# Block 0's tile masks packed four groups to a word, score masks moved between scores, and the last normalisation finished on ScalarE

## The reference

```python
# block 0
qkv = (layer_norm(x, ln1_g, ln1_b) @ Wqkv + bqkv).reshape(N, 3, H, DH)       # N = 625, H = 8, DH = 64
a = einsum('ehd,ehd->eh', q[src] * D ** -0.5, k[dst]) + dist_attn + path_attn
e = exp(a - segment_max(a, dst)[dst]); sa = e / segment_sum(e, dst)[dst]
agg = segment_sum(v[src] * sa[:, :, None], dst)
h1 = x + agg @ Wo + bo; block0 = h1 + gelu(layer_norm(h1) @ W1 + b1) @ W2 + b2
# block 1: 4 layers of sparse attention + MLP; block 2: hidden MLP and a sum over edges
# block 3: 8 attention heads over the edges, and then
x = (x + block3 - mean) / sqrt(var + 1e-5)                                     # the output, 625 x 512
```

## Time and profile before

| what | us |
|---|---|
| median of 3 runs | 1360.0 (1359.12 to 1360.21) |
| the profiled execution | 1355.65 |
| its span | 1353.7 |
| PE busy | 1161.8 (86% of the span) |
| DVE busy | 871.6 (64%) |
| POOL busy | 268.5 (20%) |
| ACT busy | 456.7 (34%) |

### The profile page before, as it was taken

How to read it: one execution, slowest core, us unless ns; L and a number is a source line. 1 busy time by engine, 2 the same in 40 slices (tenths; PEclk the granted TensorE clock), 3 DMA queues, 4 the chain that set the end, 5 groups by cost and what they waited for, 6 DMA issues and landing times.

```text
span 1353.7 us, 15095 instructions
## 1 busy us (share of the span) xinstructions
PE 1161.8 (86%) x5730; PEld 884.6 (65%) x5730; DVE 871.6 (64%) x1536; ACT 456.7 (34%) x673; POOL 268.5 (20%) x313
## 2 busy tenths in 40 slices
PE   5987845667889997899999999999999999879983
PEld 2654523334458975897779877898779877646552
DVE  6686745545644258566776667667766568937885
ACT  1010640000014432435325343336235342216780
POOL 1266338888600001000110000000110001110001
PEclk9988877788889998899999999999999999778897
DMA  6255883222151143020010201121010321000001
GB/s 181 61 150 152 278 258 81 46 52 67 18 163 56 33 130 105 4 101 25 32 62 4 101 23 63 32 65 61 31 60 3 101 62 54 16 0 1 0 1 38
DMA packets 47903, 93.95 MB, mean 69 GB/s; under 512 B 17200, under 2 KB 17600, under 8 KB 46418
## 3 DMA queue, kind: packets, MB, share of 16 engines
q1 hardware_dynamic: 27338, 71.77, 16.8%
q0 software_dynamic: 20480, 20.99, 6.5%
HBM read 74.65 MB, written 17.91 MB: 68 GB/s over the span
## 4 chain that ended last, share of the span: by engine, by line
PE 63%; DVE 14%; POOL 10%; ACT 5%; issue 4%; DMA 3%; SPq 0%; POOLq 0%; DVEq 0%; ACTq 0%
PE ps L1481 16%; PE ps L1534 15%; PE ps L1509 10%; POOL logit_ring L601 6%; PE ps L1514 5%; PE ps L1568 4%; POOL arena L595 3%; PE ps L1639 2%; PE ps L1668 2%; DMA logits_scratch<-arena 2%; PE ps L1497 2%; DVE weight_low L1171 1%; PE ps L1614 1%; DVE arena L933 1%; ACT arena L794 1%
## 5 line engine op out<-in xcount | busy, mean ns | idle before, releaser
L1481 PE MATMUL ps<-arena 125*128 125x314 f32 (+5 forms) x820 | 228.4, 459 | 11.1 <-DVE neg_max L1040 7.1
L1481 PEld LDWEIGHTS ps<-arena 125*128 125x128 f32 (+5 forms) x820 | 143.1, 188 | 85.9 <-DVE neg_max L1040 13.5
L579 POOL TENSOR_TENSOR var_eps<-mean_var,ln_consts 125x1 f32<-125x1 f32 x70 | 15.6, 222 | 919.1 <-DVE mean_var L1187 564.9
L1639 PE MATMUL ps<-arena 125*125 125x512 f32 x192 | 120.6, 722 | 68.0 <-DVE arena L1069 62.0
L595 POOL DMA_INDIRECT arena<-value_scratch,src_idx x80 | 101.6, 1270 | 72.9 <-DMA logits_scratch<-arena 32.7
L601 POOL DMA_INDIRECT logit_ring<-logits_scratch,pair_idx x80 | 107.4, 1343 | 24.4 <-issue 24.1
L1568 PE MATMUL ps<-ident,arena 125*125 125x125 f32 x625 | 81.0, 284 | 15.6 <-ACT arena L870 7.7
L1568 PEld LDWEIGHTS ps<-ident,arena 125*125 125x125 f32 x625 | 75.9, 195 | 25.0 <-ACT arena L870 8.9
L1639 PEld LDWEIGHTS ps<-arena 125*125 125x125 f32 x192 | 32.9, 215 | 70.2 <-issue 69.8
L1640 PEld LDWEIGHTS ps<-arena 125*125 125x125 f32 x192 | 40.3, 210 | 55.6 <-issue 55.6
L1509 PE MATMUL ps<-input_high,weight_high 128*128 128x314 f32 x320 | 73.0, 309 | 2.7 <-DVE weight_low L1171 2.7
(11 more groups left out here) (267 smaller groups left out, 2655.9 us busy)
## 6 DMA issues: line engine op xcount, KB each, us to landing
logits_scratch<-arena SPq DMA_DIRECT2D x5, 2187.5 KB
arena<-in_m_w SPq DMA_DIRECT2D x8, 1024.0 KB, 6.5
arena<-in_w_up SPq DMA_DIRECT2D x4, 1024.0 KB, 8.3
arena<-in_w_down SPq DMA_DIRECT2D x4, 1024.0 KB, 10.1
arena<-in_wq SPq DMA_DIRECT2D x4, 1024.0 KB, 5.2
arena<-in_wk SPq DMA_DIRECT2D x4, 1024.0 KB, 5.1
arena<-in_wv SPq DMA_DIRECT2D x4, 1024.0 KB, 5.4
arena<-in_wo SPq DMA_DIRECT2D x4, 1024.0 KB, 5.3
```

Of the source, the lines that this page charges most:

```text
L1481: last = mm(out_view[:, place:place + HALF_W], w, r[:, lo:lo + HALF_W], start=n == 0, stop=n == len(pairs) - 1 and not open_end)
L1639: mm(ps[0:TILE, 512 * j:512 * j + 512], onehot, VG[slot][:, u, :], start=False, stop=True, skip_group_check=True)
```

## The change

1. The 5-bit words of four neighbouring groups are put into one word of 20 bits (`mask_word`, four more small Vector instructions), and TensorE's stream loads a word once in four groups, in the count loop and in the message loop. The branches stay; they test another bit.
2. Of the five score masks only the first is made before the scores. Masks 1 to 4 are made on the Vector engine between the first four heads' scores and that of head 4, in tile 0.
3. In the last normalisation GpSimd makes mean times rstd after the two power instructions, ScalarE negates it and applies scale and shift to the tile, and the Vector engine's pass over the tile goes. The output is stored for tiles 0 and 1, 2 and 3, and 4 as each is ready.

```diff
@@ sync
-            sp.wait_ge(sig("out_ready"), NT)
-            node_transfer(rows_view(out), X, "out_stored")
-            sp.wait_ge(sig("out_stored"), 32)
+            for pair in PAIRS:
+                sp.wait_ge(sig("out_ready"), pair[-1] + 1)
+                tiles = slice(pair[0], pair[-1] + 1)
+                node_transfer(rows_view(out)[:, tiles, :], X[:, tiles, :], "out_stored")
+            sp.wait_ge(sig("out_stored"), 32 * len(PAIRS))
@@ gpsimd
-            for n in range(3):
+            for n in range(2):
                 powers((sig("var_ready3"), sig("rstd_ready3")), pool_chain, n * NT)
+            for t in range(NT):
+                pool.wait_ge(sig("var_ready3"), 2 * NT + t + 1)
+                pool_chain(pool, g.tensor_tensor(vare[:, t:t + 1], mv[:, t, 1:2], lnc[:, 0:1], ALU.add))
+                pool_chain(pool, g.tensor_tensor(rstd[:, t:t + 1], vare[:, t:t + 1], lnc[:, 1:2], ALU.pow))
+                g.tensor_tensor(centre[:, t:t + 1], mv[:, t, 0:1], rstd[:, t:t + 1], ALU.mult).then_inc(sig("centre_ready"), 1)
@@ scalar
+            for t in range(NT):
+                act.wait_ge(sig("centre_ready"), t + 1)
+                a.activation(shift[:, t:t + 1], centre[:, t:t + 1], ACT.Copy, scale=-1.0).then_inc(sig("shift_ready"), 1)
+                act.wait_ge(sig("shift_ready"), t + 1)
+                a.activation(X[:, t, :], X[:, t, :], ACT.Identity, bias=shift[:, t:t + 1], scale=rstd[:, t:t + 1]).then_inc(sig("out_ready"), 1)
@@ vector
-            v.tensor_copy(mask_i[:, :], mask_f[:, :]).then_inc(sig("mask_ready"), 1)
+            of_four = mask_f[:, :].rearrange("p (w k) -> p w k", k=4)
+            dve_chain(dve, v.tensor_copy(mask_word[:, :], of_four[:, :, 3]))
+            for k in (2, 1, 0):
+                dve_chain(dve, v.scalar_tensor_tensor(mask_word[:, :], mask_word[:, :], float(1 << NT), of_four[:, :, k], ALU.mult, ALU.add))
+            v.tensor_copy(mask_i[:, :], mask_word[:, :]).then_inc(sig("mask_ready"), 1)
...
-            for j in range(NT):
+            def score_mask(j):
                 dve.wait_ge(sig("counts_ready"), j + 1)
                 dve_chain(dve, v.tensor_scalar(MASK[:, j, :], C2[:, j, :], 0.5, -BIG, ALU.is_lt, ALU.mult))
-            dve.sem_inc(sig("masks_ready"), 1)
-
+
+            score_mask(0)
             for n in range(NT * H0):
                 j, h = divmod(n, H0)
+                if j == 0 and 1 <= h < NT:
+                    score_mask(h)
+                    if h == NT - 1:
+                        dve.sem_inc(sig("masks_ready"), 1)
                 A.wait_filled(dve, ("s", j, h))
...
-            norm(back, 2 * NT, X, block3_end, done=sig("out_ready"))
+            for t in range(NT):
+                block3_end(t)
+                dve_chain(dve, v.bn_stats(stats[:, t, :], X[:, t, :]))
+                v.bn_aggr(mv[:, t, :], stats[:, t, :]).then_inc(sig("var_ready3"), 1)
@@ tensor
+            def mask_of_four(group):
+                return pe.value_load(mask_i[0:1, group // 4:group // 4 + 1], min_val=0, max_val=(1 << 4 * NT) - 1)
+
+            def reached(word, group, j):
+                return (word & (1 << (NT * (group % 4) + j))) > 0
...
             for group in range(GROUPS):
-                reached = pe.value_load(mask_i[0:1, group:group + 1], min_val=0, max_val=(1 << NT) - 1)
+                if group % 4 == 0:
+                    word = mask_of_four(group)
                 pe.wait_ge(sig("onehot_ready"), group + 1)
                 for j in range(NT):
-                    with pe.If((reached & (1 << j)) > 0):
+                    with pe.If(reached(word, group, j)):
...
```

More of the change, by code:

```diff
@@ L290, in build @@
         vare = sbuf("var_eps", [TILE, NT])
+        centre = sbuf("mean_rstd", [TILE, NT])
         lnc = sbuf("ln_consts", [TILE, 2])
+        shift = sbuf("minus_mean_rstd", [TILE, NT])
         negm = sbuf("neg_max", [TILE, 2, NT])
@@ L305, in build @@
         mask_f = sbuf("group_mask_f", [1, GROUPS])
-        mask_i = sbuf("group_mask", [1, GROUPS], i32)
+        mask_word = sbuf("mask_word_f", [1, GROUPS // 4])
+        mask_i = sbuf("mask_words", [1, GROUPS // 4], i32)
         fw1 = sbuf("f_w1", [2 * NFREQ, COND])
```

## The result

| | before | after |
|---|---|---|
| timed runs, median of 3 | 1360.0 us (1359.12 to 1360.21) | 1346.05 us (1345.98 to 1346.53) |
| the profiled execution | 1355.65 | 1346.53 |
| its span | 1353.7 | 1344.7 |
| PE, DVE, ACT, POOL busy | 1161.8, 871.6, 456.7, 268.5 | 1161.8, 869.9, 462.3, 266.3 |

The changed kernel is faster: the ratio of the times on record is 0.9915, 95% interval [0.9886, 0.9944]. This ratio is an estimate of its own and not the quotient of the two medians, which is 1346.05 / 1360.0 = 0.9897.

The account below looks back on a forecast made before the run. The prediction took TensorE's instruction stream to pace the count loop, feeding block 0's chain of stores and gathers, then TensorE's own work. Terms −4.8 + 1.7 − 4.5 = −7.6 took 1360.0 to 1352.4 us, range 1349.2 to 1357.3.

Parts of the forecast that it names:

- What bounds the kernel: Block 0: TensorE's instruction stream paces the count loop; time won or lost between counts and first store reaches the gathers.
- The mask words: Count loop: fifteen fewer loads at 0.63 us, until the last one-hots limit it; −4.8 us, nothing from the message loop.
- The score masks: First scores: masks 1 to 4, now between scores, delay the first store of logits by 1.7 us net.
- The rival that the stores hide it: First stores of logits: stores, not scores, set the pace, so the masks cost nothing; 1350.7 us, chance 0.14.
- The end, flight: Last output store: 250 KB in place of 1250 KB takes 2.5 us after issue, not 5.95; −3.45 us.
- The rival of a last store that keeps its length: End of kernel: the small last store takes as long as before, the end gives only −1.5; 1355.4 us, chance 0.09.
- The end, Vector engine and ScalarE: Last normalisation: three L915 fewer save 1.65 us, the path through ScalarE adds 0.6; last store issued 1.05 us earlier.
- The rival on gathers that stretch: GpSimd's 80 logit gathers slow beside Vector work, from mean 1.343 us; at 1.50 the time is 1365.0 us; chance 0.04.
- The base, and the width of the range: Whole kernel: timed median stays 4.35 us above the profiled execution; 8-in-10 range 1349.2 to 1357.3, with 0.8 for run spread.

Follow-up runs that it names:

- the later sets: The changed kernel measured twice more without edit, beside the kernel before: 1349.67 us, ratio 0.994, and 1350.45 us, ratio 0.9939.
- the first set: Runs of the changed kernel's first repeat (1349.67 us), the words, the masks and the end alone, beside the kernel before (median 1359.34 us).

## Why the prediction missed, step by step

- **What bounds the kernel.** Right. The loads were the pace, and a shorter count loop reached the gathers: from the first count matmul to the first gather of logits it was 119.6 us and is 118.3: −4.7 of the loop, +2.0 of the masks, +1.3 from the stores to the gather and 0.1 beside. With the words alone it is 115.3.
- **The mask words.** Predicted −4.8, measured −4.7. A load is 0.63 to 0.71 us (predicted 0.63), a jump 0.41 (0.38 to 0.47), a group without a load 1.78 us, some 1.4 (about 1.9), and the loop closes 3.12 us behind the last one-hots (3.2), 4.2 to 4.3 in three later traces with the last 8 matmuls at the lower clock (2.38 us and not 1.30). The loads' whole 9.4 us didn't come, because the one-hots were late next, as said. Nothing from the message loop: its tail bears this out, but the 1.8 us between the first gather of logits and the end of the aggregation, which come with the packed words, had no term, and it is open whether they come from that loop.
- **The score masks.** Predicted +1.7, measured +2.0, with the masks alone +1.7, and +2.4 against the same kernel with the masks first (8.8 to 11.2). The rival that the stores hide it (0.14) fell: from the store to the gather it took no less than before (43.2 to 43.6 against 42.2), and no less than with the masks first (43.4 and 43.7).
- **The end, flight.** Predicted −3.45, measured 2.9 against 6.4 us, −3.5. The rival of a last store that keeps its length fell.
- **The end, Vector engine and ScalarE.** Predicted −1.05, measured −1.8: the stretch from the transposes to the last aggregate fell by 14.05 − 11.69 = 2.36, not by 1.65, and ScalarE's path took +0.54 (predicted +0.6, though its pass over a tile took 0.81 and not 0.60). The 0.7 beyond the three L915 is a mis-sized term, of which the signals are 0.55. I counted only the instructions with a row of their own. The signal inside `norm` has none; it showed in the timeline only as the pause of 0.15 us ahead of the aggregate, and it was in the code that the change replaced.
- **The rival on gathers that stretch.** It fell: the mean was 1325 ns, in later traces 1347 and 1349, before 1343.
- **The base, and the width of the range.** This is the step that failed: "The timed runs' median stands 4.35 above that execution for the same kernel, and I take the difference over". Against the profiled execution the forecast was 1348.05 and the measured one 1346.53, 1.5 lower: the end gave −0.8 and the masks +0.3; the start gave −1.4, the stores up to the gather +1.3, the gathers of logits and the aggregation's tail together −2.0, and the long middle +0.9. The start and the middle belong to the execution, since the later traces of the same kernel have other values (table above); the −2.0 is of the size of the 1.8 us that go with the packed words. The 4.35 us didn't carry over at all: the profiled execution of the changed kernel stands 0.5 above its median. In the later sets this offset was −1.8 and +1.0 for the very same kernel. It fits the place of one execution in a scatter of some 10 us, for which the range had 0.8. With the ratio of the later sets the forecast would have been met (1351.8 and 1351.7 against 1352.4); with the first it missed by 6.3 us by the medians, and by 4.0 if the recorded ratio is put to 1360.0 (1348.4). Of this 0.5 can be laid to the terms of the change, and up to 1.8 to the stretch for which the sum had none. The rest, 4.0 to 5.8 by the medians, is the level: a kernel before measured at the upper part of its scatter (1360.0, later medians 1356.9 to 1359.3) and a changed kernel measured below all its later runs. What set that level stays open. That the later ratios meet the forecast is partly luck, since the terms that were off have both signs and the scatter is larger than any of them.

The single edits add up, as far as their scatter of some 2 us each lets one say: −6.5, +0.8 and −3.9 by the medians of the first set are −9.6, and the changed kernel in that set is at −9.7.

## What to carry to other kernels

Where TensorE's idle time reads "issue" in a loop with conditional blocks, count the rows of its stream, loads of a register first, and ask which data are late next: that, and not the sum of the loads, limits the gain. When a helper's call is replaced by a written-out loop, compare every instruction of the two, semaphore increments too, since the profile shows them only as pauses. One profiled execution and three timed runs don't place the level of a kernel whose runs scatter by 0.8%: give the range that scatter, and move work that was hidden in a wait only if the new place is hidden too.

## What the runs showed of the hardware beyond that

- A value load into a register of TensorE's stream, with the two rows that come with it, took 0.63 to 0.71 us; a jump over a conditional block took 0.41.
- A semaphore increment alone on the Vector engine, between two dependent instructions, cost 0.11 us each time.
- A store of 250 KB that runs behind others ended 2.9 us after it could be issued, and 3.4 where the tile before it was ready 1.3 us ahead of it and not 2.0; one of 1250 KB took 6.4, all to the end of the span.
- ScalarE's pass over 512 elements a lane with scale and shift from a column took 0.81 us, and 0.59 for its 500-wide copies in the earlier trace rows: the row that I took for it was of another form.
- Executions of one kernel scatter by about 10 us here (the kernel before: 1352.19 to 1362.57 in 67 runs). Between traces of the changed kernel the start moves by 1.9 us, 80 gathers of logits by 2.8, and the middle by 1.8.
